# Attention in a mixed kernel: one maximum per slot over the scores of four heads, in place of two over two heads each

## The reference, cut to what matters

```python
q = (h @ wq.T + bq_).reshape(bh, sl, H, DH)
k = (h @ wk.T + bk_).reshape(bh, sl, H, DH)
scores = jnp.einsum('blhd,bmhd->bhlm', q, k) * inv_sqrt_d
w_avg = jax.nn.softmax(scores, axis=-1).mean(axis=1)
new_w = jax.nn.softmax(CSCALE * w_avg + rel[None], axis=-1)
sa = jnp.einsum('blm,bme->ble', new_w, h)
h1 = _ln(h + sa, l1w, l1b)
h2 = _ln(h1, l2w, l2b)
ff = jax.nn.relu(h2 @ w1.T + b1_) @ w2.T + b2_
return (_ln(h2 + ff, l3w, l3b), None)
```

## Time and profile before

| | |
|---|---|
| time, median of 3 runs | 2061.22 us (2057.03 to 2063.28) |
| the profiled execution | 2058.43 us |
| its span, first to last instruction | 2056.5 us |
| mean granted TensorE clock | 0.95 of full speed |
| busy: TensorE / VectorE / ScalarE / GpSimd | 1762.6 / 1661.3 / 1602.7 / 1224.6 us |
| attention stage, the scores' part | from 52 us to 1122 us of the span |

### The profile page before, as it was taken

How to read it: one execution, slowest core, us unless ns; L and a number is a source line. 1 busy time by engine, 2 the same in 40 slices (tenths; PEclk the granted TensorE clock), 3 DMA queues, 4 the chain that set the end, 5 groups by cost and what they waited for, 6 DMA issues and landing times. The chain is left out here.

```text
span 2056.5 us, 37700 instructions
## 1 busy us (share of the span) xinstructions
PE 1762.6 (86%) x9830; PEld 1327.8 (65%) x9830; DVE 1661.3 (81%) x4303; ACT 1602.7 (78%) x5245; POOL 1224.6 (60%) x2106
## 2 busy tenths in 40 slices
PE   1788998899899889989989588669994999999996
PEld 0566776677677667767767456246562777777775
DVE  3799999999999999999998432768885788777784
ACT  1798999898899999999998223489971788888884
POOL 1267776777677677677777433359884555454450
PEclk8899999999999999999999699779997999999998
DMA  2222122122212222222220321012212000000000
GB/s 79 74 76 78 73 88 77 68 80 85 73 70 89 72 75 80 84 74 74 90 75 22 112 74 43 18 62 103 93 72 79 1 1 1 1 1 2 1 1 21
DMA packets 75299, 120.50 MB, mean 59 GB/s; under 512 B 10536, under 2 KB 59952, under 8 KB 67872
## 3 DMA queue, kind: packets, MB, share of 16 engines
q1 hardware_dynamic: 65920, 109.91, 15.3%
q10 hardware_dynamic: 7920, 5.60, 1.0%
q0 software_dynamic: 1248, 2.59, 0.4%
HBM read 95.44 MB, written 24.20 MB: 58 GB/s over the span
## 5 line engine op out<-in xcount | busy, mean ns | idle before, releaser
L436 ACT ACTIVATE a_prob<-a_scores,a_negmax 128x256 f32<-128x256 f32 x1536 | 706.5, 484 | 85.3 <-DVE a_negmax L538 57.9
L538 DVE TENSOR_REDUCE a_negmax<-a_scores 128x2 f32<-128x512 f32 x768 | 518.3, 675 | 43.5 <-PE a_scores L672 43.0
L684 PE MATMUL a_heads<-a_prob,a_diag 128*128 128x256 f32 x1920 | 478.2, 389 | 40.6 <-POOL a_diag L327 40.6
L327 POOL TENSOR_TENSOR a_diag<-ident,a_rowinv 128x256 f32<-128x256 f32 (+1 forms) x384 | 280.2, 735 | 248.7 <-DVE a_rowinv L592 243.5
L684 PEld LDWEIGHTS a_heads<-a_prob,a_diag 128*128 128x128 f32 x1920 | 358.3, 195 | 96.7 <-POOL a_diag L327 51.6
L672 PE MATMUL a_scores<-a_spread,a_spread 72*128 72x256 bf16 x1536 | 265.0, 276 | 92.9 <-ACT a_prob L436 53.9
L436 ACT ACTIVATION_READ_ACCUMULATOR a_prob<-a_scores,a_negmax 128x1 f32 x1536 | 330.9, 215 | 0.0
L672 PEld LDWEIGHTS a_scores<-a_spread,a_spread 72*128 72x128 bf16 x1536 | 127.6, 98 | 213.1 <-ACT a_prob L436 102.7
L1477 DVE TENSOR_TENSOR_SCAN c_state<-c_decay,c_psD 128x1024 f32<-128x1024 f32 x64 | 146.1, 2286 | 35.8 <-PE c_psD L1594 26.5
L1309 POOL TENSOR_TENSOR c_du<-c_state,c_c_row 128x1024 f32<-128x1024 f32 x64 | 151.3, 2365 | 30.3 <-DVE c_state L1477 21.2
L1933 ACT ACTIVATE d_prob<-d_psS,d_bias 128x128 f32<-128x128 f32 (+1 forms) x256 | 99.0, 396 | 35.5 <-DVE d_bias L2064 34.6
(11 more groups left out here) (291 smaller groups left out, 4111.4 us busy)
## 6 DMA issues: line engine op xcount, KB each, us to landing
a_spread<-a_split SPq DMA_DIRECT2D x48, 576.0 KB
a_spread<-a_split SPq DMA_DIRECT2D x144, 192.0 KB
a_split<-a_parts SPq DMA_DIRECT2D x48, 384.0 KB
c_c_row<-c_rows SPq DMA_DIRECT2D x32, 512.0 KB, 3.6
b_w<-in_b_w SPq DMA_DIRECT2D x1, 2816.0 KB, 14.9
a_w<-in_a_w ACTq DMA_DIRECT2D x10, 256.0 KB, 5.4
b_w<-in_b_w SPq DMA_DIRECT2D x1, 1536.0 KB, 17.9
d_wqkv<-in_d_wqkv SPq DMA_DIRECT2D x2, 768.0 KB, 5.8
```

The costliest lines, as they stand in the source:

```text
L327: g.tensor_tensor(diag[part % RING][:], ident[:].unsqueeze(1).broadcast_to([P, len(heads), P]), rowinv[part % RING][:, heads.start:heads.s ...
L436: ins = a.activation(prob[part % RING][:, c, :], psS[part % 2][:, c, :], ACT.Exp, bias=negmax[part % 2][:, c:c + 1], accum_out=rowsum[part ...
L538: v.tensor_reduce(negmax[part % 2][:, hs], psS[part % 2][:, hs, :], AX.X, ALU.max, negate=True).then_inc(s["negmax_ready"], 1)
L684: ins = p.matmul(psH[:, t, :], diag[part % RING][:, k, :], prob[part % RING][:, c, :], start=(j == 0 and k == 0), stop=(j == HG - 1 and c ...
```

## The change

Stage a alone. The steps max0 and max1 become one step max: one reduction over the score tile's four heads (128 x 1024 in, 128 x 4 out). It waits for the scores of all four heads. ScalarE waits once, ahead of the first exponential, for that maximum. On VectorE the order inside a slot becomes invert, join, max, sum_a, sum_b. TensorE's waits and signals stay as they are, and so do `exp_done` and all other steps.

```diff
             for k in range(QSLOTS):
-                for kind in ("score", "max0", "max1"):
+                for kind in ("score", "max"):
                     place(at + k, kind, l, q, k)
...
                         a.wait_ge(s["head_done"], n - RING + 1 + RING)
+                        a.wait_ge(s["negmax_ready"], n + 1)
                         for c in range(CH):
-                            if c % BH == 0:
-                                a.wait_ge(s["negmax_ready"], n * HALVES + c // BH + 1)
                             ins = a.activation(prob[part % RING][:, c, :], psS[part % 2][:, c, :], ACT.Exp,
...
-                def negate_max(m, part, h):
+                def negate_max(m, part):
 
                     n = m * G8 + part
-                    hs = slice(h * BH, (h + 1) * BH)
-                    v.wait_ge(s["scores_ready"], (n + 2 * G8) * HALVES + h + 1)
-
-                    v.wait_ge(s["exp_done"], n * HALVES + h + 1)
-                    v.tensor_reduce(negmax[part % 2][:, hs], psS[part % 2][:, hs, :], AX.X, ALU.max,
+                    v.wait_ge(s["scores_ready"], (n + 1 + 2 * G8) * HALVES)
+
+                    v.wait_ge(s["exp_done"], (n + 1) * HALVES)
+                    v.tensor_reduce(negmax[part % 2][:], psS[part % 2][:], AX.X, ALU.max,
                                     negate=True).then_inc(s["negmax_ready"], 1)
...
-                    elif kind == "max0":
-                        negate_max(m, part, 0)
-                    elif kind == "max1":
-                        negate_max(m, part, 1)
+                    elif kind == "max":
+                        negate_max(m, part)
...
-                run(v, do, first=("invert", "join", "max0", "sum_a", "max1", "sum_b"))
+                run(v, do, first=("invert", "join", "max", "sum_a", "sum_b"))
```

## The result

The change makes the kernel slower: 2086.78 us (median of 4 runs, 2084.08 to 2089.83) beside 2062.25 us for the kernel before (4 runs, 2057.03 to 2068.46). The ratio is 1.0128, interval 1.0109 to 1.0147. The forecast was 2076 us with 2060 to 2090: the sign and the range held; the loss is 24.5 us between the medians where 15 were forecast. The profiled executions took 2088.29 us with a span of 2086.5, against 2058.43 and 2056.5 before; their difference, 29.9 us, is larger than that of the medians, because the one of before lies low among its runs and that of after high. (Ratios are measured beside the kernel before on the same chip and are not exactly quotients of the medians shown.)

A forecast was written before the change was run, and what follows sets the result against it. The bound was taken to be a ring through VectorE (busy 1,008 of 1,070 us), ScalarE and TensorE. Clean sequences 9.0 us, longer ones 5.8 and the ends 0.6 made +15 on 2061.2: 2076 us, range 2060 to 2090.

The forecast's parts named there:

- Length of the maximum: VectorE's merged 1,024-column maximum: 1.19 us, holding the queue 1.11 us where two cost 1.18, so 0.07 us saved per merger.
- the last leg: VectorE from maximum 2 to the next maximum 5: 10.05 us before, less 3 x 0.07, so 9.84 us.
- (2): A slot's first exponential on ScalarE waits for the whole maximum: starts 1.31 us after its start, not 0.78, 0.53 later.
- (3): VectorE's maximum waits for scores of four heads, not two: the wait ends 0.21 us later.
- the slack: Room before VectorE's maximum of slot 2, whose scores were ready early: 0.23 us a sequence before the change.
- (4): On VectorE sum_a moves behind the maximum, about 0.53 us later; readers two or more slots off, costed at nothing.
- the ring: Maximum 5, exp 5, ScalarE and TensorE work, maximum 2, next maximum 5: 22.16 us against 21.86, +0.30 a clean sequence.
- a merger that saves nothing: Bound on the merged maximum's length: 0.07 us longer, 0.28 us more in each sequence, so +27 us in total.
- (A): Rival, chance 0.10: VectorE's queue is the bound and the ring has hidden slack; all 27 us come off, 2034 us.
- (B): Rival, chance 0.10: no change, real slack about 0.5 us, so lateness and saving cancel; 2055 to 2067 us.
- The sum: Over 47 slot 5 distances: 30 clean 9.0 us, 11 longer 5.8, six at the ends 0.6; together +15 us.
- (C): Rival, chance 0.10: longer TensorE idle times drop its clock; four more load sequences give 2084 us, clean ones too past 2100.

## Why the prediction was right, and where it was mis-sized

- **Length of the maximum**: right. 1.19 to 1.23 us, 1,209 ns in the mean; it holds the queue 761.84 - 760.73 = 1.11 us after the reciprocal and 774.18 - 773.04 = 1.14 after a wait. So a merger saves the forecast 0.07 us, but in slot 2, where the maximum now starts out of a wait, only 0.04. That the last leg still comes to the forecast 9.84 with sum_b late is partly luck: the kernel before lost 0.06 us there to a GpSimd product (0.54 against 0.48), and the changed one does not. The price of the Trainium skill's page "VectorE: DVE Perf Modes", 120 cycles or 0.125 us for each instruction less, would make 48 us. As durations the rows agree: the group fell from 518.3 to 464.0 us, 0.14 for each merger. As time on a full queue they do not, since half of that was hidden under the neighbour.
- **(2) exp waits for the whole maximum**: right, and what the forecast's loss comes from (1.31 us; slot 5 alone merged has the forecast period within 0.02 once the clash over `rel` is allowed for; two maxima with the joined wait lose 0.73).
- **(3) the maximum waits for four heads**: right. Alone it is hidden by the slack; behind (2) it costs 12.31 - 12.08 = 0.23 us where 0.21 was taken, about what the three mergers of the last leg give back.
- **(4) sum_a moves behind the maximum, costed at nothing: the step that failed.** Its readers were searched two slots off, but in the slots that have a sum_b its first reader, sum_b, is now the very next instruction. The term should have been 2 x 0.13 = 0.26 us in the leg from maximum 2 to maximum 5. With it the sum of the ring reads 22.42, the measured period. Moving sum_b gave 22.16 back. The two waits outside that leg fall where VectorE has idle time ahead of maximum 2, and cost nothing that the period shows (12.31 us, forecast 12.32). That 2086.78 us is still inside the range is luck as far as this term goes: the range reached up to 2090 for a merger that saves nothing and for the clock.
- **(A) and (B)** fell with the forecast period of maximum 5 to maximum 2. That VectorE's queue is the bound is true of the run with sum_a first and of the one with all merged but slot 5, which have no wait for scores at maximum 2, not of this change.
- **The sum, in the profiled pair**, from the distances between slots 5: 29 clean ones grew by 16.2 us (0.56 each, forecast 0.30); the 30th, otherwise clean, grew by 3.3; the 11 longer ones by 10.5 (forecast 5.8); the six at the ends by 0.9 (forecast 0.6). Together 30.9, less some 1 us outside them, is the 29.9 of the two executions. So of the 15 us by which this pair exceeds the forecast, 0.26 us x 30 = 8 are the wait of sum_b.
- **(C) the clock**: partly so. In the stage's steady part, TensorE was granted 1.2 GHz in six stretches before and in nine after: one more inside the otherwise clean distance, two more, net, among those with weight loads. The window below takes in two of the nine; its rows stand around the second:

```profile
694.86 1.23 DVE L536 TENSOR_REDUCE a_negmax<-a_scores 128x4 f32<-128x1024 f32 x1
...
700.38 1.23 DVE L536 TENSOR_REDUCE a_negmax<-a_scores 128x4 f32<-128x1024 f32 x1 [2.58 <-PE a_scores L668]
...
670.00:700.00 30.00, 25.70 (x130) 20.34 (x129) 23.95 (x54) 23.99 (x94) 19.62 (x46) 0.89 0.23 78
```

The mean granted clock of that window is 0.89, as in the earlier trace rows, and VectorE waits 2.58 us for scores. A weight-load distance is 25.0 to 25.8 us with such a stretch and 23.3 without, 1.7 to 2.5 us apart, and the otherwise clean one is 2.7 longer, so three more are worth 5 to 8 of the 30 us of this pair. That share is read off, not tested: across the experiments the number of such stretches ran from 3 to 10 without following the total, and no run here sets it. How many of them belong to the change and how many to the execution stays open, and so does how much of the 24.5 us between the medians they are.

## What to carry to other kernels

Before two small instructions are merged, look at who starts on the signal of the first: in a ring of engines a saved 0.07 us of VectorE's queue was paid with a 0.53 us later start of the next engine, and one slot of eight decided it. Follow the ring to find where there is slack and merge only there (0.25% faster here instead of 1.3% slower). When an instruction is moved or taken out, look at its new neighbours too: what stood between a result and its reader was hiding a wait.

## What the runs showed of the hardware

- Waiting for one's own result on VectorE costs time when nothing stands between: start to start 0.52 us instead of 0.39 behind a 256-column product, 0.20 instead of 0.09 behind a reciprocal. The Trainium skill ("VectorE: DVE Perf Modes", section on the DRAIN you can't avoid) reports a test of copies in which a semaphore after each "costs nothing extra"; here the wait on one costs 0.11 to 0.13 us, and work put in between gives it back. No run has the two neighbours without the semaphore, so how much of it is the semaphore and how much the fresh result is not shown.
- An instruction of VectorE that reads two tensors of SBUF is held by a GpSimd product that is running when it starts: 0.71 us with 0.42 us of the product to go (768.22 - 767.80), 0.92 with 0.63 to go (772.04 - 771.41), 0.48 with none: the rest of the product plus 0.29, once that is more than 0.48. With one tensor of SBUF it is not held (471 to 491 ns, with up to 0.79 us of a product to go). Nor did GpSimd's products on 128 x 2 numbers hold it: 0.48 to 0.49 us in 45 cases after the change, with 0.31 to 0.37 us to go. The Trainium skill ("Advanced Engine Details and Errata", section VectorE Performance Modes) says that the second SBUF port of VectorE is shared with GpSimd and that the two "will interfere/block eachother", and names the two-port modes; what is held here is an f32 product of two SBUF tensors, written to PSUM.
